# Self loops taken out of the gathered edge lists, compacted lists built on GpSimd, and the query products moved behind the key and value products

## The reference

```
edge_index = jnp.stack([src, dst])
x = _layernorm(x + _L0_gnn_ref(x, edge_index, ...))    # four SAGE layers
x = _layernorm(x + _L1_gnn_ref(x, edge_index, ...))    # one message layer (mean)
x = _layernorm(x + _L2_gnn_ref(x, src, dst, ...))      # attention over the edges, feed-forward
x = _layernorm(x + _L3_gnn_ref(x, edge_index, ...))    # one last mean layer
...
def _L2_gnn_ref(h, src, dst, ...):
    hn = _batch_norm(h, bn1_g, bn1_b)
    Q, K, V = hn @ Wq, hn @ Wk, hn @ Wv                # 8 heads of 16
    score = clip(einsum('ehd,ehd->eh', K[src], Q[dst]) / sqrt(HD), -5, 5)
    a = softmax of score over the edges of one target
    wV = segment_sum(V[src] * a, dst)
    h2 = h + wV @ Wo + bo
    h3 = relu(_batch_norm(h2) @ W1 + b1) @ W2 + b2
    return h2 + h3
```

## Time and profile before

| what | value |
| --- | --- |
| median of 3 runs | 1321.13 us (1319.81 to 1322.5) |
| profiled execution, its own time | 1321.58 us |
| span of the profiled execution | 1319.8 us |
| PE busy | 986.8 us |
| DVE busy | 859.4 us |
| ACT busy | 519.9 us |
| POOL busy | 412.9 us |
| mean granted TensorE clock | 0.82 |

### The profile page before, as it was taken

The page is one execution under the profiler, slowest core; times in us unless marked ns, Lnnn a source line. Parts: engine busy times, 40 slices in busy tenths (PEclk is TensorE's granted clock), DMA queues, the critical chain, the costliest instruction groups (busy, mean ns, idle before and its releaser), DMA issues. The chain is left out here.

```text
span 1319.8 us, 18063 instructions
## 1 busy us (share of the span) xinstructions
PE 986.8 (75%) x6084; PEld 628.7 (48%) x6084; DVE 859.4 (65%) x2017; ACT 519.9 (39%) x1055; POOL 412.9 (31%) x514
## 2 busy tenths in 40 slices
PE   1288898989999999794666666666665666647997
PEld 1176777545555556353533444444443443424654
DVE  3887888423543466566467788887888878775343
ACT  1155555201211111111465666655666555533210
POOL 4000000000000000000277777777777777750000
PEclk9998988989999999897855667676677666657999
DMA  6020000700000000000453333333333333327111
GB/s 154 24 51 1 1 1 1 237 10 0 5 5 0 17 16 19 17 1 21 127 147 104 106 104 106 106 104 104 105 107 104 104 107 105 105 75 168 48 46 30
DMA packets 51077, 89.00 MB, mean 67 GB/s; under 512 B 13714, under 2 KB 36389, under 8 KB 50610
## 3 DMA queue, kind: packets, MB, share of 16 engines
q0 software_dynamic: 20608, 55.20, 14.5%
q1 hardware_dynamic: 27888, 31.05, 8.6%
q10 hardware_dynamic: 2492, 1.61, 0.5%
HBM read 71.83 MB, written 15.99 MB: 67 GB/s over the span
## 5 line engine op out<-in xcount | busy, mean ns | idle before, releaser
L1630 POOL DMA_INDIRECT counts_all<-kv_d,counts_all x416 | 395.7, 951 | 146.3 <-issue 139.0
L812 PE MATMUL bank<-counts_all,parts 125*128 125x500 f16 (+2 forms) x1400 | 274.9, 355 | 21.4 <-DVE parts L1077 9.7
L812 PEld LDWEIGHTS bank<-counts_all,parts 125*128 125x128 f16 x1400 | 127.6, 98 | 158.0 <-issue 13.5
L1506 POOL IOTA iota_n<- 128x256 f16 x1 | 0.3, 342 | 596.4 <-issue 596.4
L1810 PE MATMUL bank<-counts_all 125*128 125x128 f16 x1230 | 135.2, 290 | 52.7 <-ACT counts_all L1912 52.2
L1810 PEld LDWEIGHTS bank<-counts_all 125*128 125x128 f16 x1230 | 111.0, 134 | 97.5 <-ACT counts_all L1912 97.0
L1825 PE MATMUL bank<-counts_all,parts 128*128 128x272 f16 x615 | 135.4, 378 | 8.7 <-DVE counts_all L1678 6.9
L1721 DVE TENSOR_TENSOR counts_all<-counts_all,bank 128x512 f32<-128x512 f32 x104 | 71.5, 687 | 105.0 <-DMA counts_all<-kv_d,counts_all 104.8
L978 ACT CAST counts_all<-bank 125x500 f16<-125x500 f32 (+1 forms) x157 | 91.7, 594 | 85.0 <-PE bank L756 85.0
L1799 PE MATMUL bank<-rel_rows,ident_h 104*128 104x512 f16 x104 | 57.3, 551 | 79.3 <-ACT away L1902 58.8
L1902 ACT ACTIVATE away<-bank,lane_bias 125x512 f16<-125x512 f32 x173 | 110.8, 680 | 1.1 <-PE bank L1799 0.7
(11 more groups left out here) (288 smaller groups left out, 1430.4 us busy)
## 6 DMA issues: line engine op xcount, KB each, us to landing
counts_d<-counts_all SPq DMA_DIRECT2D x1, 6835.9 KB
counts_all<-kv_d,counts_all POOLq DMA_INDIRECT x416
counts_all<-counts_d SPq DMA_DIRECT2D x1, 4785.2 KB
kv_d<-counts_all SPq DMA_DIRECT2D x6, 448.0 KB
counts_all<-counts_d SPq DMA_DIRECT2D x3, 683.6 KB
inv_deg<-invdeg_d SPq DMA_DIRECT2D x1, 1562.5 KB, 6.9
q_d<-counts_all SPq DMA_DIRECT2D x1, 1562.5 KB
x<-in_x SPq DMA_DIRECT2D x6, 250.0 KB
```

What stands on the lines that cost most here:

```text
L812: last = T.matmul(agg_ps[p][:, 0:w], pin[:, s, part, :], counts[:, s, bass.ds(b * BLK, w)], start=(s + part == 0), stop=(s + part == NT))
L1630: G.indirect_dma_start(out=out_rows, out_offset=None, in_=table_d, in_offset=bass.IndirectOffsetOnAxis(ap=index, axis=0)).then_inc(signal, 16)
```

## The change

Each node has a self loop, so a self loop's row of keys and values need not be looked up: for a tile of 125 nodes they are 125 consecutive rows of `kv_d`. The change takes the self loops out of the lists. Of the 416 chunks, 391 now hold drawn edges and 25 hold one tile's self loops each (chunks 8, 24, 41, ..., 407); the number of groups stays 104. The 25 self-loop chunks are read by a plain DMA from SP (`own_rows`, signal `loops_in`), the others by POOL's gathers. No group has more than one self-loop chunk.

The lists without self loops are made on POOL, in the block of the layers, behind `built`: two halves of 98 x 2 x 208 elements are loaded and 257 instructions remove the loops and move the rest together, each waiting for the one before it in nearly all cases (`step.run`). PE then transposes the result (8 transposes, at the start of layer 4), ACT copies it, and POOL tests it and makes `att_rel` (the relative targets) in about 110 small instructions, runs of which do not wait for each other (`step.done`). The test in the setup (`glim`, `clim` and their DVE instructions) and the store of `reldst` go.

In the block of keys, values and queries all key and value products come first, the query products behind them; the query's first part is copied by ACT. POOL gathers group 0 at the end of this block, once all stores of `kv_d` have landed.

```diff
+E2 = E - N
+CHE = -(-E2 // LANES)
+CROWS, CROWG = 98, 4
+MARGIN = 34
+SPAN = 208
+CODE = 4096.0
...
+ETILES = [tiles_of(e * LANES, (e + 1) * LANES) for e in range(CHE)]
+LOOPS_BEFORE = {round((t + 0.5) * E2 / NT / LANES): t for t in range(NT)}
...
+CTILES = [[LOOPS_OF[c]] if EDGES_OF[c] is None else ETILES[EDGES_OF[c]] for c in range(CH)]
...
-                    for t_ in range(NT):
-                        of = [g for g in range(NG) if GTILES[g][0] == t_]
-                        if of:
-                            last = G.memset(glim[:, of[0]:of[-1] + 1], float(t_ * TILE))
...
-                    st.done(V.tensor_tensor(under[:, :], dstN[:, 0:CH], clim[:, 0, :], ALU.subtract))
-                    st.done(V.tensor_tensor(over[:, :], dstN[:, 0:CH], clim[:, 1, :], ALU.subtract))
...
+                        step = Steps(pool, list_step)
+                        pool.wait_ge(built, 1)
+                        step.run(G.memset(faults, 0.0))
...
+                        for half in range(2):
...
+                            pool.wait_ge(list_load, 16 * 6 * (half + 1))
+                            step.done(G.tensor_copy(p0[:, :, 0:SPAN + 1], p0.bitcast(i32)[:, :, 0:SPAN + 1]))
...
+                            for bit in range(7):
+                                k, top = 2 ** bit, float(2 ** (6 - bit))
+                                step.run(G.tensor_scalar(c_, a, top, None, ALU.is_ge))
+                                step.run(G.tensor_tensor(d_, c_, b_, ALU.mult))
+                                step.run(G.tensor_tensor(b_, b_, d_, ALU.subtract))
+                                step.run(G.tensor_tensor(b_[:, :, 0:SPAN - k], b_[:, :, 0:SPAN - k], d_[:, :, k:SPAN], ALU.add))
+                                if bit < 6:
+                                    step.run(G.tensor_tensor(c_, c_, a, ALU.mult))
+                                    step.run(G.tensor_tensor(a, a, c_, ALU.subtract))
...
+                        pool.wait_ge(by_lane_ready, 2)
...
                         for l in ls[1:]:
+                            if KINDS[l] == "message":
+                                pe.wait_ge(list_step, ROWS_STEPS)
...
+                            if KINDS[l] == "message":
+                                act.wait_ge(lists_turned, 2)
+                                S.copy(dst_by_lane, ps[6][:, 0:CROWS * CROWG]).then_inc(by_lane_ready, 1)
...
+                        pool.wait_ge(att_in, 32)
+                        pool.wait_ge(kv_out_done[0], 32 * (NBLK // 2 + 1))
+                        pool.wait_ge(kv_out_done[1], 32 * (NBLK // 2))
+                        wide = windows_spanned(ET.Pool)
+                        with pool.If(wide <= 1):
+                            for k in range(GRP):
+                                G.indirect_dma_start(out=kv[:, 0, k, :], out_offset=None, in_=kv_d,
...
-                        for g in range(NG):
+                        for g in range(1, NG):
                             if g >= RING:
                                 pool.wait_ge(va_ready, g - RING + 1)
                             for k in range(GRP):
-                                c = g * GRP + k
-                                gather(kv[:, g % RING, k, :], kv_d, srcidx[:, c:c + 1], kv_in[g % RING])
+                                e = EDGES_OF[g * GRP + k]
+                                if e is not None:
+                                    gather(kv[:, g % RING, k, :], kv_d, att_src[:, e:e + 1], kv_in[g % RING])
...
+                            if g in groups_with_loops:
+                                dve.wait_ge(loops_in, 16 * (groups_with_loops.index(g) + 1))
```

More of the change, by code:

```diff
@@ L74, with spans_of @@
 LAST_OF = [c // GRP for c in LAST_CHUNK]
+def spans_of(values):
+    spans, at = [], 0
+    for value, same in groupby(values):
+        n = len(list(same))
+        spans.append((value, at, at + n))
+        at += n
+    return spans
 SPILL = 15
@@ new lines, in _ @@
+                        step.wait()
+                        step.run(G.tensor_tensor(low, low, high, ALU.add))
+                        n_ = CHE - 1
+                        step.run(G.tensor_tensor(low[:, 0:1], low[:, 0:1], low[:, n_:n_ + 1], ALU.add))
+                        n_ //= 2
+                        step.run(G.tensor_tensor(low[:, 0:n_], low[:, 0:n_], low[:, n_:2 * n_], ALU.add))
+                        for k in range(1, 5):
+                            step.run(G.tensor_tensor(low[:, 0:39], low[:, 0:39], low[:, 39 * k:39 * (k + 1)], ALU.add))
@@ new lines, in _ @@
+                        step.run(G.tensor_tensor(faults[:, 0:39], faults[:, 0:39], low[:, 0:39], ALU.add))
+                        worst = high[:, 0:64]
+                        step.run(G.partition_all_reduce(worst, faults, 128, bass.bass_isa.ReduceOp.absmax))
+                        n_ = 64
+                        while n_ > 1:
+                            n_ //= 2
+                            step.run(G.tensor_tensor(worst[:, 0:n_], worst[:, 0:n_], worst[:, n_:2 * n_], ALU.add))
+                        step.run(G.tensor_scalar(worst[:, 0:1], worst[:, 0:1], 2.0, None, ALU.min))
@@ L1444, in build @@
             kv_in = [sem(f"kv_in{i}") for i in range(RING)]
+            loops_in = sem("loops_in")
+            groups_with_loops = [c // GRP for c in range(CH) if LOOPS_OF[c] is not None]
+            assert all(h - g >= RING for g, h in zip(groups_with_loops, groups_with_loops[1:]))
             pool_waits = sem("pool_waits")
```

259 lines of the change are left out of this document (196 added, 63 removed).

## The result

The changed kernel takes 1332.75 us (median of four runs, 1330.16 to 1334.61) against 1321.82 for the one before: a ratio of 1.0084, 95% interval 1.0062 to 1.0105. The forecast was 1298.4; the change is slower, not faster. The profiled execution takes 1330.16 us, its span 1328.4.

A forecast was written before the change was run, and what follows sets the result against it. PE was taken to bound the layers, DVE's chain their ends, and POOL's issue of gathers the attention. The sum was 1321.6 - 36.4 + 3.2 + 10 = 1298.4 us, bounds 1286.5 to 1319.4, 8-in-10 range 1286 to 1317.

The forecast's parts named there:

- The compaction's length: POOL's list-making under the layers: 184 us (94 to 253), plus about 10 for loads, from 262 to 456 us.
- PE waits for nothing: Head of layer 4: lists end at 456 us, PE needs them at 528.2, so the transposes fit its 8.06 us idle.
- Late lists: Rival, head of layer 4: DVE slows POOL, lists end at 573, PE waits 37 us, total about 1335; chance 0.12.
- What the compaction does to DVE: Ends of layers 1 and 2, plus layer 4: POOL delays DVE's norm chains, +10 us (0 to 28).
- The list of four instructions: In a layer's block, four DVE instructions use SBUF alone (L1040, L1052, L1053, L1056); POOL can delay these.
- the setup's row: Setup: a small DVE instruction took 3.18 us beside POOL's MEMSETs, another 0.16 without POOL; taken as evidence of holding up.
- The start of the gathers: Block of keys, values and queries: the last block's first gather starts at 657.7 instead of 654.45, +3.2 us (1.3 to 6.2).
- Removed gathers: Attention: 25 gathers removed and four moved earlier shorten the run by 29 x 1.256 = 36.4 us.
- the ring evens that out: Attention: self-loop groups take 3.77 us, below DVE's round; the buffers between POOL and DVE absorb this at no cost.
- POOL sets the pace, with DVE close behind: Attention: POOL issues a gather every 1.256 us and bounds the stage; DVE is 0.93 us a group behind.
- Behind the gathers: Past the last gather: 14.5 us to the next block, claimed unchanged.
- The edits in the setup: Setup: removing the test and the store of `reldst` gains nothing, as DVE's 9.32 us wait for the features covered them.

The follow-up runs named there:

- fast_all: The changed kernel with cheaper compaction instructions, the old product order without early gathers, and the store of the counts behind layer 1's loads: 1297.30 us, ratio 0.9794.
- chain_alone: The kernel before, plus the whole compaction on POOL under layers 1 to 4 with its lists unused: 1338.75 us, ratio 1.0138.
- turn_later: The changed kernel with PE's eight transposes of the lists moved from layer 4's head to behind its second block's projection: 1325.83 us, ratio 1.0034.
- forms: The kernel before, plus fourteen forms of single POOL instructions, six times each, unused, under layers 1 to 4; run once for durations: 1323.61 us.
- before_store: The kernel before, with only SP's store of the counts moved behind the loads of layer 1: 1308.80 us, ratio 0.9907.

## Why the prediction was wrong

It was 31.8 us below the profiled execution, which its own terms divide.

- **The compaction's length** (184 us, ends 94 and 253, and 10 for the second half's loads; measured 286.4 with 1.5 for these loads, from 278.26 to 564.65): the step that failed first. I priced one-input instructions by the nearest row, a MEMSET at 0.86 ns an element; the 62 large ones took 96.3 us, 1.55 each instead of 0.36, and make 74 of the 101 us. The two-input price, 2.5 ns, was near (1.11 us for 1.04), but by luck, since its row was an IOTA, which has no input. No bound held, since no row of before showed such an instruction: the bounds were those of other instructions. The start was 16 us late: the loads waited behind the store (26.66 us; 1.78 in `fast_all`), and there were 7.19 us of idle time ahead of the first two-input instruction.
- **PE waits for nothing**: it waits 22.22 us. Late lists was a rival at 0.12, but by another cause (DVE holding POOL) than the price of the instructions; that its 1335 lies near the result is luck. Beyond what DVE loses in `chain_alone`, 29.6 - 17.2 = **12.4 us** are left at the product block. This is a remainder and no measurement of lateness: it also holds the transposes and POOL's small instructions in layer 4, and `turn_later` brought 4 to 7 us of it back.
- **What the compaction does to DVE** (+10, 0 to 28): 17.2 (`chain_alone`), **+7.2**. For the ends of layers 1 and 2 I had 9, and 6.0 was measured in the changed kernel; the rest is layer 3, which I had left out because the lists were to be done, and 2.9 us in layer 4 of `chain_alone`. The mechanism, POOL holding DVE up, was right, its place followed from the wrong length. The list of four instructions that POOL can hold up was too short: layer 3's normalisation of `u` isn't in it. Nor is the setup's row a case of the two SBUF inputs cited beside it: DVE's instruction there has one, and a MEMSET only writes.
- **The start of the gathers** (+3.2): +4.9, **+1.7**. The early gathers began 24.2 us into the block, as worked out (24.7); the meeting and the flag took 4.9 us instead of 2.6.
- **Removed gathers** (-36.4): -23.5, **+12.9**. Two parts failed. The four early ones were taken for a gain of 5.0 us, but the first scores come 9.5 us behind the meeting (698.49) whatever is there, so POOL ran into a full ring and waited 7.0 us. And "the ring evens that out" was wrong by some 6 us, not for the ring's sake: groups of three move POOL's gathers under DVE's subtraction. That POOL sets the pace, with DVE close behind, held.
- **Behind the gathers**: -0.8 and -1.6, forecast 0: **-2.4**, whose cause I didn't look for.

7.2 + 12.4 + 1.7 + 12.9 - 2.4 = 31.8. The edits in the setup cost nothing, as said; no wait for `loops_in` showed.

## What to carry to other kernels

Price an instruction by its own operation on its own engine: where the trace has no such row, one run with six of each form gives it, and bounds taken from other kinds of instruction are none. Work that is put on an idle engine beside the critical one is paid twice, by its own deadline and by what it takes from its neighbour at the ends of stages, where the neighbour has no slack; and a wait's length isn't what its removal gives back (22 us of wait, 4 to 7 us gained). When one engine's period changes, look at the phase in which it now meets the others.

## What the runs showed that I had not expected

- On POOL a multiplication with an addition takes 0.54 us where either alone takes 1.25 us, for 416 elements a lane.
- POOL stands idle for some 7 us ahead of its first two-input instruction, with nothing to wait for that the profile shows: 7.19 us in the changed kernel, 6.94 in `forms`.
- DVE's subtraction with both inputs in SBUF lengthens a gather's issue on POOL from 0.95 to as much as 1.49 us. The same section of the Trainium skill's "SBUF — State Buffer" infers that such an instruction leaves the writing of DMA descriptors alone; here the gather's issue waits for its end all the same, and the measurement decides. Whether it is the writing of the descriptors that waits, or the reading of the gather's own list, no run shows.
- PE's 8.63 us without a visible cause ahead of layer 1 go when the store of 7.6 MB is issued later, and 13 us of the total with them. What in the store's company holds PE was not tried. The traces have a hint: the DMA queue q8, of the kind "instruction", moved no packet from 254 to 266 us before and two from 266 to 272, where `before_store` has two from 254 to 266. That PE waited for its own instructions is not shown.
